# Attention with its row maxima folded in pairs: four folded pairs per half head in place of three

## The reference

```python
q = (h @ W_q + b_q) @ W_s          # 2 batches, 2048 tokens, 256 channels
k, v = h @ W_k + b_k, h @ W_v + b_v
# split into 16 heads of 16 channels
scores = einsum('bhqd,bhkd->bhqk', q, k) / sqrt(16)
attn = softmax(scores, axis=-1)
out = einsum('bhqk,bhkd->bhqd', attn, v) @ W_o + b_o
x = x + ga * out
# then layer norm, a router over 8 experts with 512 tokens each, two layers, a scatter add
```

## Time and profile before

| | |
|---|---|
| median of 3 runs | 1678.5 us (1675.32 to 1684.49) |
| profiled execution | 1679.1 us, span 1677.3 us |
| TensorE matmul busy | 1627.8 us (97% of the span) |
| VectorE busy | 1462.5 us (87%) |
| ScalarE busy | 1358.3 us (81%) |
| exps (L1215) | 2048 |
| plain reductions (L1238) | 1626 |
| copies (L1201), fused operations (L1242) | 186 each |

### The profile page before, as it was taken

The page is one execution under the profiler, slowest core; times in us unless marked ns, Lnnn a source line. Parts: engine busy times, 40 slices in busy tenths (PEclk is TensorE's granted clock), DMA queues, the critical chain, the costliest instruction groups (busy, mean ns, idle before and its releaser), DMA issues. The chain is left out here.

```text
span 1677.3 us, 44152 instructions
## 1 busy us (share of the span) xinstructions
PE 1627.8 (97%) x17243; PEld 936.8 (56%) x17243; DVE 1462.5 (87%) x2913; ACT 1358.3 (81%) x2640; POOL 255.8 (15%) x323
## 2 busy tenths in 40 slices
PE   7999999999999999999999999999999997699998
PEld 5644455545555555555455555545455486488987
DVE  5679999999999999999999999999999486787783
ACT  2327999999999999999999999999999924365663
POOL 0444222100010000001000000100000012134533
PEclk9999999999999999999999999999999997699999
DMA  8771635222332233323222223342220331235332
GB/s 268 220 227 65 159 67 113 50 46 48 54 68 45 47 54 58 54 46 72 52 48 45 47 51 59 64 66 47 50 48 12 112 121 64 88 111 142 105 77 34
DMA packets 101276, 134.44 MB, mean 80 GB/s; under 512 B 27164, under 2 KB 73820, under 8 KB 97964
## 3 DMA queue, kind: packets, MB, share of 16 engines
q1 hardware_dynamic: 90444, 115.33, 30.2%
q0 software_dynamic: 7808, 14.68, 4.0%
q10 hardware_dynamic: 2816, 1.61, 0.3%
HBM read 89.64 MB, written 40.63 MB: 78 GB/s over the span
## 5 line engine op out<-in xcount | busy, mean ns | idle before, releaser
L1215 ACT ACTIVATE pt<-ps 128x512 f32<-128x512 f32 x2048 | 1074.8, 606 | 65.3 <-PE ps L699 48.3
L1238 DVE TENSOR_REDUCE pmax<-ps 128x1 f32<-128x512 f32 x1626 | 1006.9, 682 | 52.5 <-PE ps L1300 51.6
L699 PE MATMUL ps<-qp,kp 50*128 50x512 f32 x2048 | 707.0, 446 | 1.1 <-DMA qp<-m_rows 0.6
L1300 PE MATMUL ps<-kp,qp 48*128 48x512 f32 x1812 | 635.4, 448 | 0.1
L1318 PE MATMUL ps<-pt,v_st 128*32 128x256 f32 (+1 forms) x10752 | 589.6, 335 | 0.8 <-ACT pt L1215 0.7
L1300 PEld LDWEIGHTS ps<-kp,qp 48*128 48x128 f32 x1812 | 293.9, 184 | 222.3 <-DVE pmax L1238 129.4
L699 PEld LDWEIGHTS ps<-qp,kp 50*128 50x128 f32 x2048 | 330.7, 184 | 133.5 <-ACT pt L1215 115.7
L1318 PEld LDWEIGHTS ps<-pt,v_st 128*32 128x32 f32 x10752 | 265.5, 109 | 246.0 <-issue 176.1
L291 POOL CAST m_parts<-rowmax_t 128x32 fp32r<-128x32 f32 x64 | 13.4, 210 | 778.0 <-DVE rowmax_t L323 778.0
L1242 DVE CUSTOM_DVE_ANT_0 stage_b<-ps,stage_b 128x512 f32<-128x512 f32 x186 | 126.3, 679 | 0.5 <-issue 0.3
L1201 ACT ACTIVATE stage_b<-ps 128x512 f32<-128x512 f32 x186 | 114.3, 615 | 0.7 <-POOLq L1165 0.7
(11 more groups left out here) (249 smaller groups left out, 1436.1 us busy)
## 6 DMA issues: line engine op xcount, KB each, us to landing
kp<-k_parts SPq DMA_DIRECT2D x186, 128.0 KB, 4.5
v_all<-L_ffn_w SPq DMA_DIRECT2D x16, 1024.0 KB, 6.3
qp<-q_parts SPq DMA_DIRECT2D x186, 64.0 KB, 4.2
k_parts<-pt SPq DMA_DIRECT2D x16, 512.0 KB, 4.6
q_parts<-pt SPq DMA_DIRECT2D x16, 512.0 KB, 3.1
o_rows<-o_sb SPq DMA_DIRECT2D x64, 128.0 KB, 3.7
sums_c<-o_rows SPq DMA_DIRECT2D x512, 0.5 KB
kd<-kd_parts SPq DMA_DIRECT2D x186, 32.0 KB, 1.8
```

What stands on the lines that cost most here:

```text
L699: nc.tensor.matmul(bank(n % SCORE_BANKS), kp[rows, h % NBUF, kt * P:(kt + 1) * P], qp[rows, h % NBUF, f * CH:(f + 1) * CH], start=True, st ...
L1215: nc.scalar.activation(pt[:, s % PTS, half * CH:(half + 1) * CH], bank(n % SCORE_BANKS), ACT.Exp, scale=SCALE).then_inc(scores_out, 1)
L1238: v.reduce_max(pmax[:, u % 2, at:at + 1], part_slot(n), AX.X).then_inc(groups_out, 1)
L1300: mm(part_slot(n), qp[rows, r, col:col + P], keys, start=True, stop=True).then_inc(groups_full, 1)
```

## The change

The list of blocks whose last part begins a folded pair gets four members. `part_places`, `FIRSTS`, `SECONDS` and `COPY_AFTER` are worked out from it when the program is built.

```diff
@@ -58,7 +58,7 @@
 ALL_PARTS = UNITS * PARTS
 BLOCK_ORDER = "GSSGSG"
 SHORT_ORDER = "GSSG"
-FOLD_BLOCKS = (2, 5, 7)
+FOLD_BLOCKS = (2, 4, 6, 9)
 FOLD_UNIT = 2
 FOLD_CHUNK = 2
```

## The result

| | before | after |
|---|---|---|
| median of 15 runs each | 1679.58 us | 1686.27 us |
| ratio | | 1.003, 95% interval 1.0016 to 1.0043 |
| span of the profiled execution | 1677.3 us | 1683.8 us |

The change makes the kernel slower by 0.30%, 5.0 us by the ratio (2.7 to 7.2 by its interval). It was forecast at +2.7 us and "the same" within 0.5%.

The account below looks back on a forecast made before the run. TensorE was taken to run at its own pace, held only in block 7 by ScalarE's copy and exps. Stalls of +0.06 per half head, times 62, gave +3.7 us; less 1.0 for VectorE, +2.7: 1681.2 us, range 1672 to 1691.

Parts of the forecast that it names:

- ScalarE's chain of a copy and three exps: Attention stage: a third pair starts no sooner than the fold block's third exp end + 1.96 + 0.05, two blocks on.
- Outside block 7 TensorE goes at its own pace: Attention half head: blocks alternating between about 1.69 and 1.79 taken as TensorE's own; only block 7 (1.96) held, by 0.17.
- block 4's copy: New fold in block 4: the third pair of block 6 was to wait 0.08 us, ends 0 and 0.17.
- Block 6's copy: New fold in block 6: the third pair of block 8 was to wait 0.00 us, ends 0 and 0.08.
- Block 9's: New fold in block 9: block 0's third pair was to wait 0.15 us, ends 0 and 0.17.
- the old 0.17: Stall of block 7 in the kernel before, behind block 5's fold: 0.17 us per half head, to go with the change.
- VectorE's relief: Fewer reductions on VectorE, felt behind reciprocals and at the maxima's way through DRAM: -1.0 us, ends 0 and -3.6.
- rival C: Each copy behind free exps costs its full price at the third pair two blocks on: 1688 to 1693 us; chance 26%.
- A: Rival: VectorE sets the pace, so its 37 us leave the path: 1642 us; chance 4%.
- B: Rival: block 7's old stall goes and no new one comes: 1667 us; chance 8%.
- D: Rival, no change: one stall of 0.15 for one of 0.17, VectorE's gain at its far end: 1674 us; chance 14%.

## Why the prediction was right or wrong

*ScalarE's chain of a copy and three exps: right, to 0.01.* After the change block 4's third exp and the copy behind it are

```profile
807.54 0.60 ACT L1215 ACTIVATE pt<-ps 128x512 f32<-128x512 f32 x1
808.02 0.62 ACT L1201 ACTIVATE stage_b<-ps 128x512 f32<-128x512 f32 x1
```

so 808.14 + 2.01 = 810.15, and block 6's third product starts at 810.16. Block 9:

```profile
815.49 1.57 ACT L1215 ACTIVATE pt<-ps 128x512 f32<-128x512 f32 x3 [0.20 <-PE ps L699]
816.94 0.62 ACT L1201 ACTIVATE stage_b<-ps 128x512 f32<-128x512 f32 x1
```

817.06 + 2.01 = 819.07, against 819.08. The runs with the moved copy bear the chain out by the blocks in which they stall.

*"Outside block 7 TensorE goes at its own pace": wrong.* This step failed: each "due" time was read off a pattern that ScalarE itself had made. What each block has over the free pace (1.69, and 1.25 for block 2), in the two half heads shown and in the medians of all half heads:

| block | 3 | 4 | 5 | 6 | 7 | 8 | 9 | 10 | 0 | 1 | 2 | sum |
|---|---|---|---|---|---|---|---|---|---|---|---|---|
| before | 0 | 0.11 | 0.01 | 0.08 | 0.27 | -0.01 | 0.11 | 0 | 0.09 | 0.04 | 0 | 0.70 |
| after | 0 | 0.05 | 0 | 0.26 | 0.02 | 0.09 | 0 | 0.09 | 0.26 | -0.01 | 0.05 | 0.81 |
| before, medians | 0 | 0.09 | 0 | 0.09 | 0.27 | -0.01 | 0.11 | 0 | 0.09 | 0.04 | 0 | 0.68 |
| after, medians | 0 | 0.05 | 0.03 | 0.21 | 0 | 0.15 | 0 | 0.09 | 0.27 | 0 | 0.05 | 0.85 |

A stalled block costs 0.26 or 0.27, not the 0.17 of the prediction, but it isn't an addition to 1.79: it takes the place of a late load, and the blocks around it exchange theirs. In the half heads shown there are one stalled block and 0.43 in late loads before, and two and 0.29 after. By terms, there: block 4's copy was forecast at 0.08 and stalled block 6's product by 0.16, since block 4 became 1.74 in place of 1.80 and so that product was due earlier (808.64 + 1.36 = 810.00). Block 6's copy, forecast at 0, did not stall block 8 but left it a late load. Block 9's was right as a stall (0.15 forecast; due 817.55 + 1.37 = 818.92, start 819.08, 0.16). In these two half heads the sum is +0.11, in the medians +0.16, where +0.06 was forecast: 10.0 us and not 3.7.

Where the missing 0.10 lies can be told from all half heads. Counted as the prediction counts, by how late the third pair starts (free, it starts 1.36 behind its block's start), the medians are 0.11 in block 6, 0.04 in block 8 and 0.17 in block 0, where 0.08, 0.00 and 0.15 were forecast; less the old 0.17 that is +0.15. So it is the terms of the stalls that were too small, each by 0.02 to 0.04; why by so much each is known only for the half head shown. The late loads, of which the forecast knew nothing, nearly cancel: without the stalls the medians have 0.51 over the free pace before and 0.53 after.

*VectorE's relief: too small at -1.0.* The trace has -4.8 for the longer half heads. At a reciprocal block 1 now keeps 1.69 (439.20 to 440.89), where the earlier trace rows had a shifted part:

```profile
438.61 0.54 DVE L1036 RECIPROCAL sums_c<-sums_c 128x64 f32<-128x64 f32 x1
```
```profile
439.20 0.85 PE L1318 MATMUL ps<-pt,v_st 128*32 128x128 f32 x15
...
440.89 0.64 PE L1318 MATMUL ps<-pt,v_st 128*32 128x256 f32 x8
```

That part is shown for the reciprocals. The six half heads that hold them in the stage took 0.19 to 0.55 more than the median before, 1.7 us in all (0.8 to 1.2 forecast), and are within 0.05 of it now; they also are in the run with shorter reductions and in that with folds in 2, 5, 7 and 10. For the rest of the 4.8 it is not shown. The two half heads that waited for the maxima's DMA were 1.5 us longer before, and that wait went from 1.5 to 0.3 us, but the run with folds in 2, 5, 7 and 10, with as many folds, has such waits of up to 1.1 us again. The first four half heads took 2.6 us beyond the median and take 1.1, and single half heads are 0.2 to 1 us longer in most traces here, at varying places. So the forecast's number held partly by luck, because two errors of opposite sign met. In blocks the changed kernel lies between the forecast and rival C: block 7 has 1.69 (1.79 forecast), block 0 1.96 (1.93 forecast, 1.95 in C), block 6 a median of 1.90 (1.85 forecast, 1.95 in C), block 8 is held a little, as C allows and the forecast does not, and the half head has 19.01 (18.91 forecast). C's +10.5 before relief is what the pattern shows, and in the half head shown blocks 6 and 0 both have the 1.95 that the prediction had named as the sign of C.

*Rivals.* A is refuted by the shorter reductions. By the runs TensorE did have headroom, though it was busy 299.7 of 300 us: its blocks come down to 1.69 once the exps are shorter. The Trainium skill ("Perfetto Trace Analysis", Identifying the Most-Contended Engine) says that matmul busy time is not a good measure of how much is left, and these traces agree. The advice of the Trainium skill on the same page (Optimizing Scalar/DVE Operations), to give work of a saturated VectorE to ScalarE, did not help here, since it was ScalarE that the headroom waited for. B is refuted by block 0, which pays 0.27 for block 9's copy. D would have needed block 6 unhurt.

## What to carry to other kernels

Where an engine feeds another through a ring of few banks, read the round trip and not the shares: how long after the last but n-th result the next product must start, and what stands in between. An alternation of block lengths can be a sign, as here, that somebody is just too late every second time; compare the weight loads of a long and of a short block before calling any length an engine's own pace. A piece of work added to the engine in that loop costs by its place, and the place that fills a gap already there is worth more than the number of such pieces.

## What the runs showed of the hardware

Where a weight load waits for its semaphore until its product is due, the product lasts 0.48 to 0.50 and not 0.39 to 0.40 in the record, and the next group of products starts 0.42 and not 0.33 behind it, though the product itself starts on time. In these traces a load needs to be about 0.12 us ahead of its product to cost nothing. On ScalarE, from the second operation behind a gap on, the exps and the copy of a row without a gap have starts 0.477 apart, while each lasts 0.013 longer than the one before (592, 606, 618, 632, 645, 659 ns, the third of them the copy: medians in blocks 5 and 6 of the kernel before), so that their ends, which free the banks, are 0.49 apart; sums over a chain should be made with the ends.
